# A gated recurrence on one core: the low fp16 parts come from a scan instead of a subtraction

## The chip, the cores and the metric
One core of a Trainium2 chip runs the whole program. The metric is the device time in microseconds, the median of several runs. Times of single instructions come from one profiled execution. PE is TensorE, DVE is VectorE, ACT is the Scalar engine, POOL is GpSimd and SP is SyncE.

## The reference
Two layers with residual sums. The first reduces to a factor per channel, since its transform is inverted exactly: `x` becomes `x * (2 + gate)`. The second is a gated recurrence over 2048 places of two sequences, 512 channels wide. What is computed in each of the 2048 steps:

```python
z = sigmoid(xz[t] + h @ U_z + vz)
r = sigmoid(xr[t] + h @ U_r + vr)
hh = tanh(xh[t] + r * h @ U + vh)        # (r * h) @ U
h = (1.0 - z) * h + z * hh
out[t] = x[t] + h
```

## The kernel before, in words
Channels lie on the 128 partitions in K = 4 chunks, B = 2 sequences each, so a state vector is 8 numbers per partition (S = 8). It is handled in two halves of four (HS = 4, two chunks). The projections of x are made in blocks of TB = 64 steps, one block ahead, and lie in `xp`.

The recurrent products are fp16. Every fp32 value is split in a high and a low fp16 part, weights and state both. The new state is kept as the sum of two vectors, `keep = (1-z) * h` and `zn = z * tanh`, each with its own two parts, so that the product of the next r and z need not wait for their sum. `h_part` holds four parts per value, `rh_part` two. A product (`tile_product`, L252) has 128 x 128 weights and 32 streamed columns: the parts of one chunk, repeated until 32 columns are full (`WIDE`). Its sums fall into a slot of the PSUM bank. The projection of x is put into the slot's last columns by the Scalar engine (`seed`, L335 and L337). VectorE then adds up the columns of a slot (`total`, L487).

A step runs like this. PE: 32 products for r, 32 for z, 32 for h. The r products take the first half of `h_part` first (12 products) and then wait for the second half (`hs0`, `hs1`); the h products do the same with `rh_part` (`rh0`, `rh1`). DVE: reduce r; for each half `(tanh+1)*h` into fp16 (L496), the same again in fp32 (L500), and their difference, the low part (L505); reduce z and h; `keep` and its parts (L522, L523, L527); for each half `z_mul * tanh` into fp16 (L532), the same in fp32 (L536), and the low part (L541); last `h_cur = keep + zn` (L553). ACT: the tanh of each sum (L351), the copy of the state into `hist` (L363), two linear functions of z (L368, L369), the three seeds.

The order on each engine is the order of the code; engines meet by counting semaphores, and an engine also waits for its own earlier result by a semaphore. The 2048 steps are 32 blocks; a block is 4 steps with the turn of the block (`make_out`, L564, behind the first; `make_y`, L455, behind the third) and then 12 rounds of a loop with 5 steps. In each round DVE stores one slice of the next projection behind the fourth step (`store_projection`, L558), 384 times in all; its addresses depend on the round, so register instructions (L557, L558) stand ahead of it.

Of the kernel before, what the change touches and what calls it, by code (L numbers as in the profile page):

```python
# [5 lines left out]
ALU = mybir.AluOpType  # L6
# [7 lines left out]
P = 128  # L14
# [5 lines left out]
def gru_kernel(nc, x, cond, W1, b1, W2, b2, W_z, U_z, C_z, b_z, W_r, U_r, C_r, b_r, W, U, C, b, out):  # L20
# [14 lines left out]

    WIDE = 32
    SLOT = WIDE + B
    KEEP, NEW = 0, PARTS
# [7 lines left out]
    with ExitStack() as ctx:  # L46
# [54 lines left out]
        ps_r, ps_h = ([pair[:, hf, :] for hf in range(2)] for pair in (pair_r, pair_h))  # L101
        SUM, TANH = 256, 384

        def cols(bank, g, m0, m1):
            slots = bank[:, SLOT * m0:SLOT * m1].rearrange("p (m c) -> p m c", c=SLOT)
            return slots[:, :, SLOT - ADDENDS[g] * B:SLOT].rearrange("p m (a b) -> p m a b", b=B)

# [64 lines left out]
        @block.gpsimd  # L172
        def _(pool):
            nc.gpsimd.memset(ident[:, :], 0.0).then_inc(s["ident_zero"], 1)
            pool.wait_ge(s["ident_zero"], 1)
            nc.gpsimd.affine_select(out=ident[:, :], in_=ident[:, :], compare_op=ALU.not_equal, fill=1.0,
                                    base=0, pattern=[[-1, P]], channel_multiplier=1).then_inc(s["ident_ok"], 1)

            nc.gpsimd.memset(h_cur[:, :], 0.0)
            nc.gpsimd.memset(hist[:, TB:2 * TB, :], 0.0)  # L180
            nc.gpsimd.memset(y_cur[:, :, :], 0.0)
            nc.gpsimd.memset(h_part[:, 0:HC], 0.0).then_inc(s["hs0"], 1)
            nc.gpsimd.memset(h_part[:, HC:K], 0.0).then_inc(s["hs1"], 1)
            nc.gpsimd.memset(xp[:, :, TB:2 * TB, :], 0.0).then_inc(s["h0_ready"], 1)
            pool.wait_ge(s["umax_ok"], G)
            nc.gpsimd.partition_all_reduce(u_all[:, :], u_max[:, :], P, RMAX).then_inc(s["uall_ok"], 1)

        @block.tensor
        def _(pe):
# [57 lines left out]
            def tile_product(bank, m, g, gm, k, parts, first):  # L247

                n = (ADDENDS[g] - 1) * B
                moving = parts[:, k, :, :].rearrange("p a b -> p (a b)").unsqueeze(1).broadcast_to([P, WIDE // n, n])  # L250
                for part in range(PARTS):
                    last = nc.tensor.matmul(bank[:, SLOT * m:SLOT * m + WIDE].rearrange("p (r n) -> p r n", n=n),  # L252
                                            u_part[:, g, part, k, gm * P:(gm + 1) * P], moving,
                                            start=first and part == 0, stop=False, skip_group_check=True)
                return last
# [65 lines left out]
        def _(act):  # L321
# [9 lines left out]
            def seed(banks, g, at):  # L331

                src = xp[:, g * K:(g + 1) * K, at, :]
                if g == Z:
                    return A(cols(banks, Z, 0, K)[:, :, ADDENDS[Z] - 1, :], src, ACT.Copy)  # L335
                to = banks[:, :, 0:SLOT * HC].rearrange("p h (m c) -> p h m c", c=SLOT)
                return A(to[:, :, :, WIDE:SLOT], src.rearrange("p (h m) b -> p h m b", h=2), ACT.Copy)  # L337

# [14 lines left out]
            def steps(t0, count, ring, turn=None):  # L353

                for u in range(count):
# [7 lines left out]
                    A(hist[:, prv, :], h_cur[:, :], ACT.Copy)  # L363
                    tanh(th_z[:, :], ps_z, Z, S, "z_sum", t1, "z_th")
# [25 lines left out]
            act.wait_ge(s["h_ok"], T)  # L390
            A(hist[:, (T - 1) % (2 * TB), :], h_cur[:, :], ACT.Copy).then_inc(s["copied"], 1)
            put_out(NB + 1)

        @block.vector
        def _(dve):
# [94 lines left out]
            def step(t1):  # L490
                kc = (slice(0, HC), slice(HC, K))


                def gated_high(hf):
                    dve.wait_ge(s[f"r{hf}_th"], t1)
                    V.scalar_tensor_tensor(rh_part[:, kc[hf], 0, :], kb(ps_r[hf][:, TANH:TANH + HS]), 1.0,  # L496
                                           kb(h_cur[:, half[hf]]), ALU.add, ALU.mult)

                def gated_full(hf):
                    V.scalar_tensor_tensor(rh[:, half[hf]], ps_r[hf][:, TANH:TANH + HS], 1.0, h_cur[:, half[hf]],  # L500
                                           ALU.add, ALU.mult).then_inc(s[f"rh32_{hf}"], 1)

                def gated_low(hf):
                    dve.wait_ge(s[f"rh32_{hf}"], t1)
                    V.tensor_tensor(rh_part[:, kc[hf], 1, :], kb(rh[:, half[hf]]), rh_part[:, kc[hf], 0, :],  # L505
                                    ALU.subtract).then_inc(s[f"rh{hf}"], 1)

                for hf in range(2):
                    dve.wait_ge(s[f"r{hf}_mm"], t1)
                    total(ps_r[hf], R, HC, f"r{hf}_sum")  # L510

                for hf in range(2):
                    gated_high(hf)
                    gated_full(hf)
# [7 lines left out]
                V.tensor_tensor(h_part[:, :, KEEP, :], kb(z_keep[:, :]), kb(h_cur[:, :]), ALU.mult)  # L522
                V.tensor_tensor(keep[:, :], z_keep[:, :], h_cur[:, :], ALU.mult).then_inc(s["keep_ok"], 1)  # L523

                def keep_low():
                    dve.wait_ge(s["keep_ok"], t1)
                    V.tensor_tensor(h_part[:, :, KEEP + 1, :], kb(keep[:, :]), h_part[:, :, KEEP, :], ALU.subtract)  # L527


                def new_high(hf):  # L530
                    dve.wait_ge(s[f"h{hf}_th"], t1)
                    V.tensor_tensor(h_part[:, kc[hf], NEW, :], kb(z_mul[:, half[hf]]),  # L532
                                    kb(ps_h[hf][:, TANH:TANH + HS]), ALU.mult)

                def new_full(hf):
                    V.tensor_tensor(zn[:, half[hf]], z_mul[:, half[hf]], ps_h[hf][:, TANH:TANH + HS],  # L536
                                    ALU.mult).then_inc(s[f"zn{hf}"], 1)
# [77 lines left out]
```

## Time and profile before

| | us |
|---|---|
| median of 3 runs | 6809.69 (6809.19 to 6810.33) |
| profiled execution, its time | 6811.76 |
| profiled execution, its span | 6809.9 |
| PE busy with products | 5998.4 (88%) |
| DVE busy | 4955.6 (73%) |
| ACT busy | 3331.6 (49%) |
| TensorE clock granted, mean | 0.996 of full speed |

Busy time is counted per engine as the time in which at least one of its instructions is under way. Instructions of one engine overlap: the next starts some 70 to 80 ns after the one before, while each lasts 150 ns or more, so a share of 73% does not mean that a quarter of the time is free for more of them. An instruction that needs the result of the one before has to wait for its end.

### The profile page before, as it was taken

How to read it: one execution, taken by the hardware profiler on the slowest of the kernel's cores; microseconds unless marked ns; L12 is line 12 of the kernel's file. 1: busy time of each engine (PE TensorE's matmuls, PEld its weight loads, DVE VectorE, ACT ScalarE, POOL GpSimd, SP SyncE). 2: the span in 40 equal slices, each digit the busy share in tenths (PEclk: the TensorE clock that was granted, in tenths of full speed). 3: DMA queues.
4: the chain of work that ended last, by engine and by line, in shares of the span. 5: the costliest groups of instructions: out<-in, count | busy, mean ns of one | idle time of the engine just before them, and what ended most of it. 6: DMA issues, size and time to landing. Idle time of an engine off the chain costs nothing.

```text
span 6809.9 us, 488240 instructions
## 1 busy us (share of the span) xinstructions
PE 5998.4 (88%) x200232; PEld 5642.2 (83%) x200232; DVE 4955.6 (73%) x43503; ACT 3331.6 (49%) x22603; POOL 3.5 (0%) x13
## 2 busy tenths in 40 slices
PE   7888888888888888888888888888888888888888
PEld 7888888888888888888888888888888888888888
DVE  5777777777777777777777777777777777777777
ACT  3444444444444444444444444444444444444444
POOL 0000000000000000000000000000000000000000
PEclk8999999999999999999999999999999999999999
DMA  2000000000000000000000000000000000000000
GB/s 84 17 18 15 18 17 18 17 17 17 18 17 18 15 18 17 18 18 15 18 17 18 17 18 15 18 17 18 17 17 17 18 17 18 15 18 18 17 18 15
DMA packets 80315, 129.97 MB, mean 19 GB/s; under 512 B 12336, under 2 KB 18480, under 8 KB 80304
## 3 DMA queue, kind: packets, MB, share of 16 engines
q1 hardware_dynamic: 80304, 129.81, 5.5%
q8 instruction: 8, 0.13, 0.0%
q14 instruction: 3, 0.02, 0.0%
HBM read 20.46 MB, written 8.65 MB: 4 GB/s over the span
## 4 chain that ended last, share of the span: by engine, by line
PE 71%; DVE 26%; issue 3%; SPq 0%; DMA 0%; ACT 0%; ACTq 0%; DVEq 0%
PE pair_r L252 30%; PE ps_z L252 24%; PE pair_h L252 17%; DVE pair_h L487 8%; DVE h_part L522 5%; DVE h_part L541 4%; DVE h_part L527 2%; DVE keep L523 2%; DVE zn L536 2%; DVE h_part L532 2%; PE ps_z L212 0%; DMA u_raw<-in_L_cond_U 0%; PE ps_o L212 0%; DVE u_max L424 0%; PE ps_x L224 0%
## 5 line engine op out<-in xcount | busy, mean ns | idle before, releaser
L252 PEld LDWEIGHTS pair_r<-h_part,u_part 128*128 128x128 f16 x65536 | 1845.1, 96 | 1119.9 <-DVE h_part L541 1115.8
L252 PE MATMUL pair_r<-h_part,u_part 128*128 128x32 f16 x65536 | 2048.7, 177 | 771.1 <-DVE h_part L541 758.6
L252 PE MATMUL pair_h<-rh_part,u_part 128*128 128x32 f16 x65536 | 2016.6, 177 | 12.5 <-DVE rh_part L505 12.5
L252 PE MATMUL ps_z<-h_part,u_part 128*128 128x32 f16 x65536 | 1961.5, 176 | 0.0
L252 PEld LDWEIGHTS pair_h<-rh_part,u_part 128*128 128x128 f16 x65536 | 1842.8, 96 | 17.3 <-DVE rh_part L505 15.7
L252 PEld LDWEIGHTS ps_z<-h_part,u_part 128*128 128x128 f16 x65536 | 1795.3, 95 | 0.0
L487 DVE TENSOR_REDUCE pair_r<-pair_r 128x4 f32<-128x20 f32 x4096 | 759.4, 186 | 818.1 <-PE pair_r L252 615.1
L351 ACT ACTIVATE pair_r<-pair_r 128x4 f32<-128x4 f32 x4096 | 644.8, 158 | 1445.1 <-DVE pair_r L487 1182.4
L487 DVE TENSOR_REDUCE pair_h<-pair_h 128x4 f32<-128x12 f32 x4096 | 717.7, 175 | 665.7 <-PE pair_h L252 665.7
L351 ACT ACTIVATE th_z<-ps_z 128x8 f32<-128x8 f32 x2048 | 364.1, 178 | 1046.0 <-DVE ps_z L487 1046.0
L337 ACT ACTIVATE pair_h<-xp 128x8 f32 (+1 forms) x2049 | 369.9, 181 | 807.8 <-DVE zn L536 807.8
L505 DVE TENSOR_TENSOR rh_part<-rh,rh_part 128x4 f16<-128x4 f32 x4096 | 662.2, 162 | 141.1
L541 DVE TENSOR_TENSOR h_part<-zn,h_part 128x4 f16<-128x4 f32 x4096 | 669.6, 163 | 70.5
L224 PE MATMUL ps_p<-y_next,w_stage 128*128 128x128 f32 x3072 | 718.1, 316 | 0.0
L351 ACT ACTIVATE pair_h<-pair_h 128x4 f32<-128x4 f32 x4096 | 647.2, 158 | 102.2
L496 DVE SCALAR_TENSOR_TENSOR rh_part<-pair_r,h_cur 128x4 f16<-128x4 f32 x4096 | 649.6, 159 | 6.0
L532 DVE TENSOR_TENSOR h_part<-z_mul,pair_h 128x4 f16<-128x4 f32 x4096 | 625.6, 153 | 0.0
L500 DVE SCALAR_TENSOR_TENSOR rh<-pair_r,h_cur 128x4 f32<-128x4 f32 x4096 | 621.8, 152 | 0.0
L536 DVE TENSOR_TENSOR zn<-z_mul,pair_h 128x4 f32<-128x4 f32 x4096 | 619.8, 151 | 0.0
L224 PEld LDWEIGHTS ps_p<-y_next,w_stage 128*128 128x128 f32 x3072 | 458.2, 188 | 0.0
L363 ACT ACTIVATE hist<-h_cur 128x8 f32 x2048 | 428.2, 209 | 4.4
L487 DVE TENSOR_REDUCE ps_z<-ps_z 128x8 f32<-128x40 f32 x2048 | 421.8, 206 | 0.0
(70 smaller groups left out, 3275.9 us busy)
## 6 DMA issues: line engine op xcount, KB each, us to landing
w_stage<-w_in SPq DMA_DIRECT2D x384, 256.0 KB, 2.3
x_tok<-in_x SPq DMA_DIRECT2D x68, 128.0 KB, 2.6
out_dram<-o_tok SPq DMA_DIRECT2D x66, 128.0 KB, 2.3
mlp_w<-in_L_cond_W SPq DMA_DIRECT2D x2, 1024.0 KB, 6.9
u_raw<-in_L_cond_U_r SPq DMA_DIRECT2D x1, 1024.0 KB, 5.6
u_raw<-in_L_cond_U_z SPq DMA_DIRECT2D x1, 1024.0 KB, 7.6
u_raw<-in_L_cond_U SPq DMA_DIRECT2D x1, 1024.0 KB, 10.3
w_in<-in_L_cond_W_r SPq DMA_DIRECT2D x4, 256.0 KB, 9.8
```

The lines of the kernel that those rows point to most:

```text
L224: return nc.tensor.matmul(bank[:, col:col + P], weight[:, k, :], y_next[:, k * B:(k + 1) * B, :].rearrange("p b t -> p (b t)"), start=(k = ...
L252: last = nc.tensor.matmul(bank[:, SLOT * m:SLOT * m + WIDE].rearrange("p (r n) -> p r n", n=n), u_part[:, g, part, k, gm * P:(gm + 1) * P] ...
L337: return A(to[:, :, :, WIDE:SLOT], src.rearrange("p (h m) b -> p h m b", h=2), ACT.Copy)
L351: A(to, bank[:, SUM:SUM + n], ACT.Tanh, scale=scale_reg[g]).then_inc(s[done], 1)
L363: A(hist[:, prv, :], h_cur[:, :], ACT.Copy)
L487: return V.tensor_reduce(bank[:, SUM:SUM + m * B].rearrange("p (m b) -> p m b", b=B), cols(bank, g, 0, m).rearrange("p m a b -> p m b a"), ...
L496: V.scalar_tensor_tensor(rh_part[:, kc[hf], 0, :], kb(ps_r[hf][:, TANH:TANH + HS]), 1.0, kb(h_cur[:, half[hf]]), ALU.add, ALU.mult)
L500: V.scalar_tensor_tensor(rh[:, half[hf]], ps_r[hf][:, TANH:TANH + HS], 1.0, h_cur[:, half[hf]], ALU.add, ALU.mult).then_inc(s[f"rh32_{hf}" ...
L505: V.tensor_tensor(rh_part[:, kc[hf], 1, :], kb(rh[:, half[hf]]), rh_part[:, kc[hf], 0, :], ALU.subtract).then_inc(s[f"rh{hf}"], 1)
L532: V.tensor_tensor(h_part[:, kc[hf], NEW, :], kb(z_mul[:, half[hf]]), kb(ps_h[hf][:, TANH:TANH + HS]), ALU.mult)
L536: V.tensor_tensor(zn[:, half[hf]], z_mul[:, half[hf]], ps_h[hf][:, TANH:TANH + HS], ALU.mult).then_inc(s[f"zn{hf}"], 1)
L541: V.tensor_tensor(h_part[:, kc[hf], NEW + 1, :], kb(zn[:, half[hf]]), h_part[:, kc[hf], NEW, :], ALU.subtract).then_inc(s[f"hs{hf}"], 1)
```

## The change
The low part is no longer made from a full fp32 product minus the high part. Three places (a step of the scan each) stand for one value. A scan runs over them: state = state * factor - subtrahend. For the new state the factors of one value are 0, tanh and z_mul, and the subtrahends are -1, 0 and the high part, so that the states are 1, tanh and tanh * z_mul - high. For the gated state they are 0, tanh, h and -1, -1, high, which gives (tanh + 1) * h - high. The parts keep this layout in memory: `part_of` is a part with 12 places of one half, of which every third holds a value. `h_cur` and `z_mul` become columns of the factor arrays `r_scan` and `n_scan`, and the tanh results go there, into SBUF instead of PSUM. The fp32 `rh` is gone. `zn` is made once in full behind the last scan, and `h_cur` waits for it. A product streams 8 neighbouring places of each part, of which two hold values (places 2 and 5 of 8); a slot is 40 columns wide, and `total` and `seed` pick columns 2 and 5 of each run of 8. ACT's seed of `pair_h` no longer waits for `zn1`.

```diff
-    WIDE = 32
-    SLOT = WIDE + B
+    STEP, RUN, WIDE = 3, 8, 32
+    SLOT = WIDE + RUN
+    PITCH = HS * STEP
...
+        r_scan = sb("r_scan", [P, S, STEP])
+        n_scan = sb("n_scan", [P, S, STEP])
+        h_cur, z_mul = r_scan[:, :, STEP - 1], n_scan[:, :, STEP - 1]
+        h_part = sb("h_part", [P, 2 * 2 * PARTS * PITCH + RUN], F16)
+        rh_part = sb("rh_part", [P, 2 * PARTS * PITCH + RUN], F16)
...
         def cols(bank, g, m0, m1):
-            slots = bank[:, SLOT * m0:SLOT * m1].rearrange("p (m c) -> p m c", c=SLOT)
-            return slots[:, :, SLOT - ADDENDS[g] * B:SLOT].rearrange("p m (a b) -> p m a b", b=B)
+            runs = bank[:, SLOT * m0:SLOT * m1].rearrange("p (m a c) -> p m a c", c=RUN, m=m1 - m0)
+            return runs[:, :, SLOT // RUN - ADDENDS[g]:, STEP - 1:STEP * B:STEP]
...
+        def part_of(parts, count, hf, part):
+            at = (hf * count + part) * PITCH
+            return parts[:, at:at + PITCH]
+        def place(parts, count, hf, part, step=STEP - 1):
+            return part_of(parts, count, hf, part).rearrange("p (s c) -> p s c", c=STEP)[:, :, step]
...
-                n = (ADDENDS[g] - 1) * B
-                moving = parts[:, k, :, :].rearrange("p a b -> p (a b)").unsqueeze(1).broadcast_to([P, WIDE // n, n])
+                n = ADDENDS[g] - 1
+                at = k // HC * n * PITCH + k % HC * B * STEP
+                runs = parts[:, at:at + n * PITCH].rearrange("p (a c) -> p a c", c=PITCH)[:, :, 0:RUN]
+                moving = runs.unsqueeze(1).broadcast_to([P, WIDE // (n * RUN), n, RUN])
...
-                        tanh(ps_r[hf][:, TANH:TANH + HS], ps_r[hf], R, HS, f"r{hf}_sum", t1, f"r{hf}_th")
+                        tanh(r_scan[:, half[hf], 1], ps_r[hf], R, HS, f"r{hf}_sum", t1, f"r{hf}_th")
...
-                    tanh(ps_h[1][:, TANH:TANH + HS], ps_h[1], H, HS, "h1_sum", t1, "h1_th")
-                    act.wait_ge(s["zn1"], t1)
+                    tanh(n_scan[:, half[1], 1], ps_h[1], H, HS, "h1_sum", t1, "h1_th")
                     seed(pair_h, H, nxt)
...
+                def low(parts, count, hi, hf, factors, done):
+                    V.tensor_tensor_scan(part_of(parts, count, hf, hi + 1), factors[:, half[hf]].rearrange("p s c -> p (s c)"),
+                                         part_of(parts, count, hf, hi), 0.0, ALU.mult, ALU.subtract).then_inc(s[done], 1)
...
-                def gated_full(hf):
-                    V.scalar_tensor_tensor(rh[:, half[hf]], ps_r[hf][:, TANH:TANH + HS], 1.0, h_cur[:, half[hf]],
-                                           ALU.add, ALU.mult).then_inc(s[f"rh32_{hf}"], 1)
...
                 new_high(0)
-                new_full(0)
                 keep_low()
                 new_low(0)
                 new_high(1)
-                new_full(1)
                 new_low(1)
-                V.tensor_tensor(h_cur[:, :], keep[:, :], zn[:, :], ALU.add).then_inc(s["h_ok"], 1)
+                V.tensor_tensor(zn[:, :], z_mul, n_scan[:, :, 1], ALU.mult).then_inc(s["zn_ok"], 1)
+                dve.wait_ge(s["zn_ok"], t1)
+                V.tensor_tensor(h_cur, keep[:, :], zn[:, :], ALU.add).then_inc(s["h_ok"], 1)
```

VectorE from the reduction of the second half of h to the next step, in the step with `store_projection`, before (ISA and REGISTER_ALU are register instructions):

```order
L487 TENSOR_REDUCE pair_h<-pair_h 128x4 [waits s_h1_mm]
L532 TENSOR_TENSOR h_part<-z_mul,pair_h 128x2x2 [waits s_h0_th]
L536 TENSOR_TENSOR zn<-z_mul,pair_h 128x4
L527 TENSOR_TENSOR h_part<-keep,h_part 128x4x2 [waits s_keep_ok]
L541 TENSOR_TENSOR h_part<-zn,h_part 128x2x2 [waits s_zn0]
L532 TENSOR_TENSOR h_part<-z_mul,pair_h 128x2x2 [waits s_h1_th]
L536 TENSOR_TENSOR zn<-z_mul,pair_h 128x4
L541 TENSOR_TENSOR h_part<-zn,h_part 128x2x2 [waits s_zn1]
L553 TENSOR_TENSOR h_cur<-keep,zn 128x8
L557 ISA
L558 ISA [waits s_proj_mm]
L558 TENSOR_TENSOR xp<-ps_p,v_bias 128x2x64
```

The same place after the change (the scans are listed as SCALAR_TENSOR_TENSOR of L522, `h_cur` as r_scan, tanh and `z_mul` as n_scan):

```order
L514 TENSOR_REDUCE pair_h<-pair_h 128x4 [waits s_h1_mm]
L557 TENSOR_TENSOR h_part<-n_scan 128x4 [waits s_h0_th]
L552 TENSOR_TENSOR h_part<-keep,h_part 128x2x4 [waits s_keep_ok]
L522 SCALAR_TENSOR_TENSOR h_part<-n_scan,h_part 128x12 [waits s_nhi0]
L557 TENSOR_TENSOR h_part<-n_scan 128x4 [waits s_h1_th]
L522 SCALAR_TENSOR_TENSOR h_part<-n_scan,h_part 128x12 [waits s_nhi1]
L571 TENSOR_TENSOR zn<-n_scan 128x8
L573 TENSOR_TENSOR r_scan<-keep,zn 128x8 [waits s_zn_ok]
L577 ISA
L578 ISA [waits s_proj_mm]
L578 TENSOR_TENSOR xp<-ps_p,v_bias 128x2x64
```

Two instructions of four elements are gone, one of eight has come behind the second scan, and the sum `h_cur` (L553, now L573) has got a wait for it, with the register instructions behind.

VectorE in the same step, the r gate, before (`rh_part` is what the h products wait for):

```order
L496 SCALAR_TENSOR_TENSOR rh_part<-pair_r,h_cur 128x2x2 [waits s_r0_th]
L500 SCALAR_TENSOR_TENSOR rh<-pair_r,h_cur 128x4
L505 TENSOR_TENSOR rh_part<-rh,rh_part 128x2x2 [waits s_rh32_0]
L496 SCALAR_TENSOR_TENSOR rh_part<-pair_r,h_cur 128x2x2 [waits s_r1_th]
L500 SCALAR_TENSOR_TENSOR rh<-pair_r,h_cur 128x4
L505 TENSOR_TENSOR rh_part<-rh,rh_part 128x2x2 [waits s_rh32_1]
```

And after:

```order
L527 SCALAR_TENSOR_TENSOR rh_part<-r_scan 128x4 [waits s_r0_th]
L522 SCALAR_TENSOR_TENSOR rh_part<-r_scan,rh_part 128x12 [waits s_rhi0]
L527 SCALAR_TENSOR_TENSOR rh_part<-r_scan 128x4 [waits s_r1_th]
L522 SCALAR_TENSOR_TENSOR rh_part<-r_scan,rh_part 128x12 [waits s_rhi1]
```

Each half has one instruction less; the scan waits for the fp16 high part instead of the fp32 product.

## Rows read from the trace of the kernel before

**Rows 1.** Section 4 of the page: the chain that ended last, by engine and line

```profile
PE 71%; DVE 26%; issue 3%; SPq 0%; DMA 0%; ACT 0%; ACTq 0%; DVEq 0%
```

**Rows 2.** Waits: who waited for whom, us in total, times, longest us

```profile
PE pair_r L252 <- DVE h_part L541: 758.6, 1983, 0.7
```

**Rows 3.** Timeline of a step: start, length (us), engine, line, instruction [idle before <- releaser]

```profile
3001.89 1.00 PE L252 MATMUL pair_r<-h_part,u_part 128*128 128x32 f16 x32 [0.65 <-DVE h_part L541]
...
3004.59 0.17 DVE L487 TENSOR_REDUCE pair_h<-pair_h 128x4 f32<-128x12 f32 x1
...
3004.80 0.16 ACT L351 ACTIVATE pair_h<-pair_h 128x4 f32<-128x4 f32 x1
...
3004.92 0.16 DVE L541 TENSOR_TENSOR h_part<-zn,h_part 128x4 f16<-128x4 f32 x1
...
3005.14 1.00 PE L252 MATMUL pair_r<-h_part,u_part 128*128 128x32 f16 x32 [0.31 <-DVE h_part L541]
3005.26 0.16 DVE L541 TENSOR_TENSOR h_part<-zn,h_part 128x4 f16<-128x4 f32 x1
...
3005.35 0.18 ACT L337 ACTIVATE pair_h<-xp 128x8 f32 x1 [0.39 <-DVE zn L536]
...
3005.99 0.96 PE L252 MATMUL ps_z<-h_part,u_part 128*128 128x32 f16 x32
...
3006.29 0.16 DVE L496 SCALAR_TENSOR_TENSOR rh_part<-pair_r,h_cur 128x4 f16<-128x4 f32 x1
...
3006.56 0.16 DVE L505 TENSOR_TENSOR rh_part<-rh,rh_part 128x4 f16<-128x4 f32 x1
...
3006.80 0.85 PE L252 MATMUL pair_h<-rh_part,u_part 128*128 128x32 f16 x27
```

**Rows 4.** Groups of instructions by form: busy us, mean ns | idle before

```profile
L252 PE MATMUL pair_r<-h_part,u_part 128*128 128x32 f16 x65536 | 2048.7, 177 | 771.1 <-DVE h_part L541 758.6 <-issue 3.9
L252 PE MATMUL pair_h<-rh_part,u_part 128*128 128x32 f16 x65536 | 2016.6, 177 | 12.5 <-DVE rh_part L505 12.5
...
L487 DVE TENSOR_REDUCE pair_h<-pair_h 128x4 f32<-128x12 f32 x4096 | 717.7, 175 | 665.7 <-PE pair_h L252 665.7
L541 DVE TENSOR_TENSOR h_part<-zn,h_part 128x4 f16<-128x4 f32 x4096 | 669.6, 163 | 70.5
L351 ACT ACTIVATE pair_h<-pair_h 128x4 f32<-128x4 f32 x4096 | 647.2, 158 | 102.2
...
L487 DVE TENSOR_REDUCE ps_z<-ps_z 128x8 f32<-128x40 f32 x2048 | 421.8, 206 | 0.0
L351 ACT ACTIVATE th_z<-ps_z 128x8 f32<-128x8 f32 x2048 | 364.1, 178 | 1046.0 <-DVE ps_z L487 1046.0
...
L564 DVE SCALAR_TENSOR_TENSOR oT<-hist,y_cur 128x512 f32<-128x512 f32 x33 | 35.8, 1085 | 0.4 <-ACT hist L391 0.4
L455 DVE TENSOR_TENSOR y_next<-ps_x,gate 128x512 f32<-128x512 f32 x33 | 22.6, 684 | 0.2 <-PE ps_x L194 0.2
```

**Rows 5.** Timeline of a step with L558 behind it

```profile
3014.92 1.00 PE L252 MATMUL pair_r<-h_part,u_part 128*128 128x32 f16 x32 [0.30 <-DVE h_part L541]
3015.03 0.16 DVE L541 TENSOR_TENSOR h_part<-zn,h_part 128x4 f16<-128x4 f32 x1
3015.11 0.16 DVE L553 TENSOR_TENSOR h_cur<-keep,zn 128x8 f32<-128x8 f32 x1
...
3015.51 0.29 DVE L558 TENSOR_TENSOR xp<-ps_p,v_bias 128x128 f32 x1 [0.24 <-issue]
3015.72 0.42 DVE L487 TENSOR_REDUCE pair_r<-pair_r 128x4 f32<-128x20 f32 x2
...
3018.26 0.32 PE L252 MATMUL pair_r<-h_part,u_part 128*128 128x32 f16 x6 [0.64 <-DVE h_part L541]
```

**Rows 6.** Register instructions of L557 and L558 there: count, ns min/median/max, first and last start

```profile
L557 DVEq FUSED_REGOPS  x1: 114/114/114, 3015.0 to 3015.0; - x1
...
L558 DVEq FUSED_REGOPS  x2: 52/112/173, 3015.2 to 3015.4; - x2
```

More of the change, by code:

```diff
@@ L121, in gru_kernel, with keep_place @@
         half = (slice(0, HS), slice(HS, S))
+        by_half = lambda a: a.rearrange("p (h s) -> p h s", h=2)
+        def part_of(parts, count, hf, part):
[3 more added lines that the diff above has]
+            return part_of(parts, count, hf, part).rearrange("p (s c) -> p s c", c=STEP)[:, :, step]
+        def keep_place(low):
+            both = h_part[:, 0:2 * 2 * PARTS * PITCH].rearrange("p (h a s c) -> p h a s c", h=2, a=2 * PARTS, c=STEP)
+            return both[:, :, KEEP + low, :, STEP - 1]
         BYTES = 16 * B
@@ L177, in _ @@
                                     base=0, pattern=[[-1, P]], channel_multiplier=1).then_inc(s["ident_ok"], 1)
-            nc.gpsimd.memset(h_cur[:, :], 0.0)
+            nc.gpsimd.memset(r_scan[:, :, :], 0.0)
+            nc.gpsimd.memset(n_scan[:, :, :], 0.0)
+            nc.gpsimd.memset(rh_part[:, :], 0.0).then_inc(s["rh_zero"], 1)
+            nc.gpsimd.memset(h_part[:, :], 0.0).then_inc(s["scan_zero"], 1)
+            pool.wait_ge(s["rh_zero"], 1)
+            for hf in range(2):
+                for step in range(STEP - 1):
+                    nc.gpsimd.memset(place(rh_part, PARTS, hf, 0, step), -1.0)
             nc.gpsimd.memset(hist[:, TB:2 * TB, :], 0.0)
             nc.gpsimd.memset(y_cur[:, :, :], 0.0)
-            nc.gpsimd.memset(h_part[:, 0:HC], 0.0).then_inc(s["hs0"], 1)
-            nc.gpsimd.memset(h_part[:, HC:K], 0.0).then_inc(s["hs1"], 1)
+            pool.wait_ge(s["scan_zero"], 1)
+            for hf in range(2):
+                nc.gpsimd.memset(place(h_part, 2 * PARTS, hf, NEW, 0), -1.0).then_inc(s[f"hs{hf}"], 1)
             nc.gpsimd.memset(xp[:, :, TB:2 * TB, :], 0.0).then_inc(s["h0_ready"], 1)
@@ L247, in tile_product @@
             def tile_product(bank, m, g, gm, k, parts, first):
[L249 to L250 removed]
+                n = ADDENDS[g] - 1
+                at = k // HC * n * PITCH + k % HC * B * STEP
+                runs = parts[:, at:at + n * PITCH].rearrange("p (a c) -> p a c", c=PITCH)[:, :, 0:RUN]
+                moving = runs.unsqueeze(1).broadcast_to([P, WIDE // (n * RUN), n, RUN])
                 for part in range(PARTS):
[L252 removed]
+                    last = nc.tensor.matmul(bank[:, SLOT * m:SLOT * m + WIDE].rearrange("p (r a c) -> p r a c", a=n, c=RUN),
                                             u_part[:, g, part, k, gm * P:(gm + 1) * P], moving,
@@ L336, in seed @@
                 to = banks[:, :, 0:SLOT * HC].rearrange("p h (m c) -> p h m c", c=SLOT)
-                return A(to[:, :, :, WIDE:SLOT], src.rearrange("p (h m) b -> p h m b", h=2), ACT.Copy)
+                return A(to[:, :, :, WIDE + STEP - 1:WIDE + STEP * B:STEP],
+                         src.rearrange("p (h m) b -> p h m b", h=2), ACT.Copy)
             act.wait_ge(s["h0_ready"], 1)
@@ L360, in steps @@
                     for hf in range(2):
-                        tanh(ps_r[hf][:, TANH:TANH + HS], ps_r[hf], R, HS, f"r{hf}_sum", t1, f"r{hf}_th")
-                    A(hist[:, prv, :], h_cur[:, :], ACT.Copy)
+                        tanh(r_scan[:, half[hf], 1], ps_r[hf], R, HS, f"r{hf}_sum", t1, f"r{hf}_th")
+                    A(hist[:, prv, :], h_cur, ACT.Copy)
                     tanh(th_z[:, :], ps_z, Z, S, "z_sum", t1, "z_th")
@@ L368, in steps @@
                     A(z_keep[:, :], th_z[:, :], ACT.Copy, scale=-0.5, bias=0.5).then_inc(s["z_keep"], 1)
-                    A(z_mul[:, :], th_z[:, :], ACT.Copy, scale=H_SCALE / 2, bias=H_SCALE / 2)
-                    tanh(ps_h[0][:, TANH:TANH + HS], ps_h[0], H, HS, "h0_sum", t1, "h0_th")
+                    A(z_mul, th_z[:, :], ACT.Copy, scale=H_SCALE / 2, bias=H_SCALE / 2)
+                    tanh(n_scan[:, half[0], 1], ps_h[0], H, HS, "h0_sum", t1, "h0_th")
                     seed(ps_z, Z, nxt)
-                    tanh(ps_h[1][:, TANH:TANH + HS], ps_h[1], H, HS, "h1_sum", t1, "h1_th")
-                    act.wait_ge(s["zn1"], t1)
+                    tanh(n_scan[:, half[1], 1], ps_h[1], H, HS, "h1_sum", t1, "h1_th")
                     seed(pair_h, H, nxt)
@@ L390, in _ @@
             act.wait_ge(s["h_ok"], T)
-            A(hist[:, (T - 1) % (2 * TB), :], h_cur[:, :], ACT.Copy).then_inc(s["copied"], 1)
+            A(hist[:, (T - 1) % (2 * TB), :], h_cur, ACT.Copy).then_inc(s["copied"], 1)
             put_out(NB + 1)
@@ L490, in step @@
             def step(t1):
-                kc = (slice(0, HC), slice(HC, K))
+                def low(parts, count, hi, hf, factors, done):
+                    V.tensor_tensor_scan(part_of(parts, count, hf, hi + 1), factors[:, half[hf]].rearrange("p s c -> p (s c)"),
+                                         part_of(parts, count, hf, hi), 0.0, ALU.mult, ALU.subtract).then_inc(s[done], 1)
                 def gated_high(hf):
                     dve.wait_ge(s[f"r{hf}_th"], t1)
-                    V.scalar_tensor_tensor(rh_part[:, kc[hf], 0, :], kb(ps_r[hf][:, TANH:TANH + HS]), 1.0,
-                                           kb(h_cur[:, half[hf]]), ALU.add, ALU.mult)
-                def gated_full(hf):
-                    V.scalar_tensor_tensor(rh[:, half[hf]], ps_r[hf][:, TANH:TANH + HS], 1.0, h_cur[:, half[hf]],
-                                           ALU.add, ALU.mult).then_inc(s[f"rh32_{hf}"], 1)
+                    V.scalar_tensor_tensor(place(rh_part, PARTS, hf, 0), r_scan[:, half[hf], 1], 1.0,
+                                           h_cur[:, half[hf]], ALU.add, ALU.mult).then_inc(s[f"rhi{hf}"], 1)
                 def gated_low(hf):
-                    dve.wait_ge(s[f"rh32_{hf}"], t1)
-                    V.tensor_tensor(rh_part[:, kc[hf], 1, :], kb(rh[:, half[hf]]), rh_part[:, kc[hf], 0, :],
-                                    ALU.subtract).then_inc(s[f"rh{hf}"], 1)
+                    dve.wait_ge(s[f"rhi{hf}"], t1)
+                    low(rh_part, PARTS, 0, hf, r_scan, f"rh{hf}")
                 for hf in range(2):
@@ L513, in step @@
                     gated_high(hf)
-                    gated_full(hf)
                     gated_low(hf)
@@ L521, in step @@
                 dve.wait_ge(s["z_keep"], t1)
-                V.tensor_tensor(h_part[:, :, KEEP, :], kb(z_keep[:, :]), kb(h_cur[:, :]), ALU.mult)
-                V.tensor_tensor(keep[:, :], z_keep[:, :], h_cur[:, :], ALU.mult).then_inc(s["keep_ok"], 1)
+                V.tensor_tensor(keep_place(0), by_half(z_keep[:, :]), by_half(h_cur), ALU.mult)
+                V.tensor_tensor(keep[:, :], z_keep[:, :], h_cur, ALU.mult).then_inc(s["keep_ok"], 1)
                 def keep_low():
                     dve.wait_ge(s["keep_ok"], t1)
-                    V.tensor_tensor(h_part[:, :, KEEP + 1, :], kb(keep[:, :]), h_part[:, :, KEEP, :], ALU.subtract)
+                    V.tensor_tensor(keep_place(1), by_half(keep[:, :]), keep_place(0), ALU.subtract)
                 def new_high(hf):
                     dve.wait_ge(s[f"h{hf}_th"], t1)
[L532 to L537, printed above, removed]
+                    V.tensor_tensor(place(h_part, 2 * PARTS, hf, NEW), z_mul[:, half[hf]],
+                                    n_scan[:, half[hf], 1], ALU.mult).then_inc(s[f"nhi{hf}"], 1)
                 def new_low(hf):
-                    dve.wait_ge(s[f"zn{hf}"], t1)
-                    V.tensor_tensor(h_part[:, kc[hf], NEW + 1, :], kb(zn[:, half[hf]]), h_part[:, kc[hf], NEW, :],
-                                    ALU.subtract).then_inc(s[f"hs{hf}"], 1)
+                    dve.wait_ge(s[f"nhi{hf}"], t1)
+                    low(h_part, 2 * PARTS, NEW, hf, n_scan, f"hs{hf}")
                 dve.wait_ge(s["h1_mm"], t1)
```

9 lines of the change are left out of this document (2 added, 7 removed).

## The prediction
> **What bounds the kernel now.** Read the chain of waits first [rows 1]: TensorE holds 71% of it and VectorE 26%, and nearly all of it lies in the recurrence, so this is a loop of 2048 dependent steps and no engine is full. The waits say where the loop closes: the r products wait for VectorE L541, 1983 times and 758.6 us in all, 0.37 us a step [rows 2]. L541 is the low-part subtraction that the change replaces.
>
> The timeline of a step [rows 3] gives the lengths. The r products start at 3001.89 and again at 3005.14, so a step is 3.25 to 3.26 us. Between them the PE runs 32 r, 32 z and 32 h products. z takes 3005.99 to 3006.80, 0.81 us, which is 25 ns a product; r takes 0.85. The 0.04 more are two short waits in r: one after its first product, one at the thirteenth, where the second half's L541 is needed. That L541 starts at 3005.26, ends 0.16 later and reaches the PE 0.06 later (the first L541, 3004.92, ends at 5.08, and r starts at 5.14), so at 3005.48; undisturbed, the thirteenth product would be due 0.31 after 3005.14 (the first takes 0.04, eleven more 25 ns each), at 3005.45. The second half therefore closes the loop, and what is gained there is gained in all 2048 steps: the time is linear in it.
>
> The page's other stretch is a step in which VectorE does something besides the step [rows 5]. Behind the last L541 (3015.03) and h_cur (3015.11) stands L558, which starts only at 3015.51, after 0.24 us of "issue". The next reduction of r comes at 3015.72 instead of 0.07 earlier, and the next r products start at 3018.26, not 3.26 but 3.34 us after 3014.92. This happens 384 times.
>
> **Low part by scan.** In the second half now: reduce h1, tanh, high part (L532), the fp32 copy (L536), 0.03 of semaphore, L541. After: reduce, tanh, high part, semaphore, scan. L536 leaves; but the fp16 high part is now what the scan waits for. Step by step from rows 3 and 4:
> - The reduction L487 starts at 3004.59 behind L522 and L523, which now read h_cur with a gap of two words. L564 reads hist in steps of eight words and takes 1085 ns, L455 reads straight and takes 684 ns, both for 512 elements: hopping costs up to 0.78 ns an element. Sixteen elements of two instructions make at most 12 ns, no gap makes 0; I take 8. Start at 4.60.
> - L487 lasts 0.17 and tanh starts at 4.77+0.03, as now (4.80). Its target moves from PSUM to SBUF. The nearest rows are th_z (178 ns, 8 elements, into SBUF) and the same tanh into PSUM (158 ns, 4 elements); take 3 ns off for the elements and it is 16 dearer, between 0 and 20. tanh ends at 4.60+0.17+0.03+0.175 = 4.98 (unrounded).
> - High part at 5.01; both inputs are in SBUF, as in L541, hence its 163 ns. Its result is usable at 5.01+0.165+0.035 = 5.21.
> - Scan of 12 elements. No row shows one. Lower end: L541's 163 plus eight more elements at the reduction's slope ((206-175)/28 = 1.1 ns) = 172. Upper end: 12 places that each cost a triple pass, like the 40-element reduction: 206. Each place multiplies, then subtracts, and the next needs the result, so I count twice 1.1 ns: 163-4+26 = 185, which is also near the middle.
> - Scan ends at 5.21+0.185 = 5.40, and the PE has it at 5.455. Now it is 5.48. Gain 25 ns a step, 2048 x 25 = 51 us. The ends of the scan alone make it 78 us (172) and 8 us (206).
> The Trainium skill, "DVE: opcode table, instruction layouts, handler registers and perf-mode slots", section Datapath and trigger behaviour, says that the built-in scan runs at half throughput because its feedback costs bubble cycles. By that rule the scan would be 163-4 plus 12 times two cycles, 184 ns, and the sum within 2 us of mine; a rule at full rate would give 172. No row here shows a scan.
>
> The first half is not the limit: its high part is issued 0.08 behind the reduction (the spacing of L541 and h_cur in rows 5), at 4.68; 0.20 later, 4.88, its scan starts, ends at 5.065, r starts at 5.125, and the thirteenth product would be due 0.31 later, at 5.435, still before 5.455. The r gate has cover: rh must reach the PE at 3006.80; L496 at 6.29 becomes 6.31 (tanh into SBUF), +0.20, +0.185, +0.06 = 6.75, now 6.56+0.16+0.06 = 6.78. The reset of pair_h loses its wait (ACT L337 at 3005.35 behind L536); the Scalar engine then waits for r anyway, so nothing is gained. The POOL memsets and the other layout lie in the prologue, beside it: 0.
>
> **What moves late.** The fp32 product zn is no longer a by-product. Now h_cur is issued 0.08 behind the last L541 and waits for nothing. After the change the full zn (8 elements) comes 0.08 behind the last scan, and h_cur waits for it (s_zn_ok): 0.08+0.165+0.03 = 0.28 behind the scan. In 2048 steps that alone is hidden, since r's reduction is due some 0.6 us behind L541 (3015.65 against 3015.03, [rows 5]). Not hidden is what is queued behind h_cur. For L558 these are three register instructions (114, 173 and 52 ns, [rows 6]). Their first starts at 3015.0, before h_cur at 3015.11: they run past h_cur while it stands in the queue, but not past L541, which waits for a semaphore. In the same way the Scalar engine's L337, which needs a register instruction after its wait for L536, starts at 3005.35, while L541, which waits for the same and needs none, is at 3005.26. So I take it that a register instruction is held behind an instruction that waits. Then the registers start with h_cur, not with L541: from L541 to L558 it is 0.48 now; from the scan it will be 0.28+0.47 = 0.75, so 0.27 more, and the scan starts 0.045 earlier than L541: L558 comes 0.225 later on the clock. Against a step that is due 0.025 earlier, that is 0.25 later, on top of the 0.07 that L558 holds r's reduction up already: 0.32. Take off the 0.05 of cover of the r gate, and 0.27 goes through to the next step; today 0.085 does (3.34 against 3.25 to 3.26), so 0.18 more. 384 x 0.18 = 69 us. Behind make_out and make_y (L564 and L455, 33 each, of which 32 stand in the loop) the same thing happens: 64 x 0.18 = 12 us.
>
> **Sum.** Profiled execution 6811.8 us (span 6809.9 and 1.9 around it): -51 +69 +12 = +30, 6842. The three timed runs have their median 2 us lower, 6809.7: 6840 us.
>
> **Rivals.**
> (a) Faster: the register instructions run while h_cur waits. Then L558 comes out as now, and the loss is gone: 6810-51+2 = 6761 us. For it: nothing shows an instruction with a wait as the second in the queue. Against: rows 3 and 6 as above. A variant ends the same way: the loss is there but the scan costs under 165 ns.
> (b) Slower by more: strides in PSUM. All reductions now read in steps of eight words where they read in steps of two. If these cost 0.78 ns an element as in SBUF, the z reduction (40 elements, on the loop) costs 31 ns and h's (12) 9: 2048 x 40 = +82 on top of the forecast, 6922 us. For it: L564. Against: the reductions read in steps of two words already, never two neighbours in a row, and go at 1.1 ns. The Trainium skill, "PSUM — Partial Sum Buffer", section Specifications (TRN2), gives cachelines of 8 bytes and says non-contiguous patterns slow matmuls; by it the old pattern would be as bad as the new, and the time would not change; the trace's 1.1 ns agrees that two-word steps are free.
> (c) The products slow down: each now streams four runs of 8 places that begin at multiples of 12 bytes. If each took 1 ns more, the 52 products from r's thirteenth to z's last cost 52 ns a step: +106 on top, 6946 us. Against: a product of 32 columns takes 177 ns for runs of 8 (r) and for runs of 4 (h) alike [rows 4].
> (d) No change: the scan at its lower end, 172: -78+81 = +3, 6813 us.
>
> **Chances.** Forecast mechanism 0.60 (own range 6813 to 6883, -78 or -8 for the scan's ends and +81), a 0.13, b 0.13, c 0.04, d 0.10. The range of 8 in 10 reaches from 6785 (a is left out) to 6930 (c is left out). About 0.2%, 14 us, can be told from no change. Faster: a and a little of the mix, 0.18. Within: d and the lower part of the forecast, 0.22. Slower: 0.60.
>
> **What would show it.** Right: a scan of about 185 ns; the r products 3.23 us apart in plain steps; in the steps behind L558 (new number L578) some 3.49 us; h_cur about 0.28 behind the last scan, and L578 about 0.47 behind h_cur. Wrong: a scan over 206 ns, which alone makes every step longer; a z reduction over 220 ns (b); products further apart than 25 ns (c); L578 less than 0.2 behind h_cur (a).

## The result and the profile after

The changed kernel takes 6909.5 us (median of 4 runs, 6906.99 to 6911.27) against 6809.9 before: 1.0145 times, 95% interval 1.013 to 1.0161. It is slower, by 99.6 us. The forecast was +30 us, 6840, with a range from 6785 to 6930: the side was right, the size was three times too small.

The forecast's own terms first. The groups of instructions after, with the columns of [rows 4]:

```profile
L279 PE MATMUL pair_r<-h_part,u_part 128*128 128x32 f16 x65536 | 2059.7, 179 | 672.4 <-DVE h_part L522 664.8 <-issue 3.9
L279 PE MATMUL pair_h<-rh_part,u_part 128*128 128x32 f16 x65536 | 1984.6, 179 | 68.0 <-DVE rh_part L522 13.7
...
L522 DVE TENSOR_TENSOR_SCAN h_part<-n_scan,h_part 128x12 f16<-128x12 f32 x4096 | 749.8, 183 | 70.0
...
L514 DVE TENSOR_REDUCE pair_h<-pair_h 128x4 f32<-128x12 f32 x4096 | 722.2, 176 | 678.3 <-PE pair_h L279 678.3
L379 ACT ACTIVATE n_scan<-pair_h 128x4 f32<-128x4 f32 x4096 | 718.5, 175 | 140.1
...
L514 DVE TENSOR_REDUCE ps_z<-ps_z 128x8 f32<-128x40 f32 x2048 | 410.5, 200 | 1.3
```

The scan takes 183 ns (estimated 185), tanh into SBUF 175 (estimated 158+16). The reductions in eight-word steps are no dearer: 176 and 200 ns against 175 and 206 in [rows 4].

A plain step and the step behind L578, timeline (start, length, engine, line, instruction):

```profile
3001.83 1.01 PE L279 MATMUL pair_r<-h_part,u_part 128*128 128x32 f16 x32 [0.30 <-DVE h_part L522]
...
3005.06 1.01 PE L279 MATMUL pair_r<-h_part,u_part 128*128 128x32 f16 x32 [0.30 <-DVE h_part L522]
...
3008.30 1.01 PE L279 MATMUL pair_r<-h_part,u_part 128*128 128x32 f16 x32 [0.30 <-DVE h_part L522]
3008.40 0.18 DVE L522 TENSOR_TENSOR_SCAN h_part<-n_scan,h_part 128x12 f16<-128x12 f32 x1
3008.50 0.15 DVE L571 TENSOR_TENSOR zn<-n_scan 128x8 f32<-128x8 f32 x1
3008.68 0.17 DVE L573 TENSOR_TENSOR r_scan<-keep,zn 128x8 f32<-128x8 f32 x1
...
3009.16 0.29 DVE L578 TENSOR_TENSOR xp<-ps_p,v_bias 128x128 f32 x1 [0.31 <-issue]
3009.37 0.26 DVE L514 TENSOR_REDUCE pair_r<-pair_r 128x4 f32<-128x20 f32 x2
...
3011.80 0.99 PE L279 MATMUL pair_r<-h_part,u_part 128*128 128x32 f16 x32 [0.60 <-DVE h_part L522]
```

Plain steps are 3.23 us, as forecast. h_cur (now named r_scan, L573) comes 0.28 behind the scan, L578 comes 0.48 behind h_cur, the first of its register instructions starts with h_cur (row below; 14 ns behind it in every round of the trace, 64 ns ahead of it in the kernel before), and the step takes 3008.30 to 3011.80, 3.50 us (forecast 3.49); [rows 5] had 3.34.

```profile
L577 DVEq FUSED_REGOPS  x1: 114/114/114, 3008.7 to 3008.7; - x1
```

What the forecast did not have follows one step later, at the head of the loop. The timeline goes on, with the register instructions of VectorE's loop (L604) below it:

```profile
3011.89 0.18 DVE L522 TENSOR_TENSOR_SCAN h_part<-n_scan,h_part 128x12 f16<-128x12 f32 x1
...
3012.18 0.17 DVE L573 TENSOR_TENSOR r_scan<-keep,zn 128x8 f32<-128x8 f32 x1
...
3012.73 0.29 DVE L514 TENSOR_REDUCE pair_r<-pair_r 128x4 f32<-128x20 f32 x2 [0.39 <-PE pair_r L279]
```

```profile
L604 DVEq ALU_OP  x1: 40/40/40, 3012.2 to 3012.2; - x1
L604 DVEq COMPARE_BRANCH  x1: 56/56/56, 3012.3 to 3012.3; - x1
L604 DVEq FUSED_REGOPS  x1: 139/139/139, 3012.5 to 3012.5; - x1
```

In a plain step the reduction comes 0.75 us behind the r products (3005.81 against 3005.06 in the trace), here 0.93 (3012.73 against 3011.80). The branch stands behind h_cur as L578 does; the next register instruction starts 0.29 us behind the branch's start, lasts 0.14, and only then comes the reduction. In the kernel before, the step that starts at 3001.89 in [rows 3] is such a head; its branch and third register instruction are the rows below, with the same 0.29 between their starts, and its reduction comes at 3002.62, 0.73 behind the products as in any step. There the branch had just enough time.

```profile
L584 DVEq COMPARE_BRANCH  x1: 56/56/56, 3002.1 to 3002.1; - x1
L584 DVEq FUSED_REGOPS  x1: 139/139/139, 3002.4 to 3002.4; - x1
```

Then the clock. The mean granted clock is 0.937 of full speed, 0.996 before. Three stretches of TensorE, columns: us, busy us (and count) of PE, PEld, DVE, ACT, POOL, granted clock, DMA:

```profile
3041.90:3045.31 3.41, 2.69 (x99) 2.48 (x96) 2.44 (x20) 1.51 (x11) 0.00 (x0) 1.00 0.20 77
3045.31:3048.73 3.42, 3.42 (x104) 3.13 (x102) 2.38 (x19) 1.60 (x11) 0.00 (x0) 0.50 0.00 0
3048.73:3062.38 13.65, 12.03 (x415) 11.26 (x412) 10.09 (x74) 6.11 (x44) 0.00 (x0) 1.00 0.00 0
```

The stretch ahead of the fall holds the step behind L578, with PE busy 2.69 of 3.41 us. Then the clock is at its lower level, 1.2 instead of 2.4 GHz, for 3.4 us. There are 241 stretches at this level in the trace, nearly all of 3.4 us, against 3 before. 215 of them begin in the step right behind a step with L578: 184 at the head of the loop, and 31 in the first step of a block. A product takes 188 ns in them instead of 177, and a 128-column fp32 one 492 instead of 316. A step at the loop's head takes 3.40 us where the clock is at its lower level for a part of it (207 of 384) and 3.36 where it is not, and the step behind it 3.25 and 3.20.

From the start of the r products of all steps, the 99 us come together like this (mean ns of a step, and us for all of its kind):

| step of a round | count | before | after | us |
|---|---|---|---|---|
| third and fourth | 768 | 3258 | 3235 | -18 |
| fifth, behind the store | 383 | 3341 | 3510 | +65 |
| first, head of the loop | 384 | 3258 | 3385 | +49 |
| second | 384 | 3258 | 3227 | -12 |
| four at the block's turn | 128 | | | +15 |

### The profile page after: what moved, and what is told of

Read it like the earlier page. It is cut to its first block, busy times and chain, and to the rows that moved or that the text cites. A ratio compares the mean times of both kernels' runs of the same rounds, so it can differ in the third digit from the quotient of the medians.

```text
span 6909.4 us, 482103 instructions
## 1 busy us (share of the span) xinstructions
PE 6143.6 (89%) x200232; PEld 5706.4 (83%) x200232; DVE 5107.5 (74%) x37359; ACT 3188.9 (46%) x22603; POOL 3.8 (0%) x20
## 4 chain that ended last, share of the span: by engine, by line
PE 62%; DVE 30%; issue 5%; DVEq 1%; ACT 1%; SPq 0%; DMA 0%
PE pair_r L279 23%; PE ps_z L279 19%; PE pair_h L279 18%; DVE pair_h L514 7%; DVE h_part L522 5%; DVE h_part L547 4%; DVE h_part L557 3%; DVE h_part L552 2%; PE ps_p L249 2%; DVE keep L548 2%; DVE rh_part L522 1%; DVE pair_r L514 1%; DVEq L578 1%; ACT r_scan L379 1%; DVE rh_part L527 1%
## 5 line engine op out<-in xcount | busy, mean ns | idle before, releaser
L379 ACT ACTIVATE r_scan<-pair_r 128x4 f32<-128x4 f32 x4096 | 653.9, 176 | 2405.7 <-DVE pair_r L514 2250.7
L522 DVE TENSOR_TENSOR_SCAN rh_part<-r_scan,rh_part 128x12 f16<-128x12 f32 x4096 | 748.6, 183 | 140.2
L522 DVE TENSOR_TENSOR_SCAN h_part<-n_scan,h_part 128x12 f16<-128x12 f32 x4096 | 749.8, 183 | 70.0
L379 ACT ACTIVATE n_scan<-pair_h 128x4 f32<-128x4 f32 x4096 | 718.5, 175 | 140.1
L527 DVE SCALAR_TENSOR_TENSOR rh_part<-r_scan 128x4 f16<-128x4 f32 x4096 | 681.3, 166 | 120.7 <-ACT r_scan L379 74.9
L557 DVE TENSOR_TENSOR h_part<-n_scan 128x4 f16<-128x4 f32 x4096 | 684.5, 167 | 0.0
L391 ACT ACTIVATE hist<-r_scan 128x8 f32 x2048 | 435.7, 213 | 2.8
L397 ACT ACTIVATE n_scan<-th_z 128x8 f32<-128x8 f32 x2048 | 401.9, 196 | 0.0
L573 DVE TENSOR_TENSOR r_scan<-keep,zn 128x8 f32<-128x8 f32 x2048 | 349.5, 171 | 70.5
L396 ACT ACTIVATE z_keep<-th_z 128x8 f32<-128x8 f32 x2048 | 393.7, 192 | 0.0
```

What stands on the lines that cost most here:

```text
L379: A(to, bank[:, SUM:SUM + n], ACT.Tanh, scale=scale_reg[g]).then_inc(s[done], 1)
L391: A(hist[:, prv, :], h_cur, ACT.Copy)
L397: A(z_mul, th_z[:, :], ACT.Copy, scale=H_SCALE / 2, bias=H_SCALE / 2)
L522: V.tensor_tensor_scan(part_of(parts, count, hf, hi + 1), factors[:, half[hf]].rearrange("p s c -> p (s c)"), part_of(parts, count, hf, hi ...
L527: V.scalar_tensor_tensor(place(rh_part, PARTS, hf, 0), r_scan[:, half[hf], 1], 1.0, h_cur[:, half[hf]], ALU.add, ALU.mult).then_inc(s[f"rh ...
L557: V.tensor_tensor(place(h_part, 2 * PARTS, hf, NEW), z_mul[:, half[hf]], n_scan[:, half[hf], 1], ALU.mult).then_inc(s[f"nhi{hf}"], 1)
```

## The experiments

**The full zn ahead of the last scan.** The scan waits 0.2 us for its high part; zn fits in there.

```diff
-                new_low(1)
                 V.tensor_tensor(zn[:, :], z_mul, n_scan[:, :, 1], ALU.mult).then_inc(s["zn_ok"], 1)
+                new_low(1)
                 dve.wait_ge(s["zn_ok"], t1)
```

> The changed kernel with the full fp32 zn issued ahead of the last scan, in the shadow of the scan's own wait, so that h_cur's wait is met when its turn comes. Theory (register instructions are held behind h_cur's unmet wait, at L578 and at the head of the loop, and the longer TensorE pauses bring the half clock): both costs vanish, 2048 steps gain 25 ns each, 6755 to 6785 us, granted clock back at 0.99 or more, steps behind the store below 3.35 us. Rival (the hopping strides, the new streams or the scan bring the half clock by themselves): plain steps stay at 3.23, but the clock stays near 0.94 and the time above 6800 us.

Measured: 6739.9 us against 6804.9, ratio 0.9903 (0.9887 to 0.992): faster than both, and 15 us below the expected range. Its timeline:

```profile
3005.37 0.16 DVE L570 TENSOR_TENSOR zn<-n_scan 128x8 f32<-128x8 f32 x1
3005.39 1.01 PE L279 MATMUL pair_r<-h_part,u_part 128*128 128x32 f16 x32 [0.29 <-DVE h_part L522]
3005.49 0.18 DVE L522 TENSOR_TENSOR_SCAN h_part<-n_scan,h_part 128x12 f16<-128x12 f32 x1
3005.59 0.15 DVE L573 TENSOR_TENSOR r_scan<-keep,zn 128x8 f32<-128x8 f32 x1
...
3008.62 1.01 PE L279 MATMUL pair_r<-h_part,u_part 128*128 128x32 f16 x32 [0.30 <-DVE h_part L522]
```

h_cur is 0.10 behind the scan instead of 0.28, plain steps are 3.23 as in the changed kernel, the step behind the store is 3.30, the head of the loop has no excess (3.21), the clock is 0.996. The steps behind the store gain 42 ns on the kernel before and the heads 46, where plain steps gain the expected 25; why these two gain more was not tried. One instruction in another place takes back all that the change lost; scan, layout and strides are cleared.

**The wait alone.** As above, but h_cur waits for the last scan, which it does not need.

```diff
+                t2 = dve.snap(t1 + 1)
                 dve.wait_ge(s["z_mm"], t1)
...
+                V.tensor_tensor(zn[:, :], z_mul, n_scan[:, :, 1], ALU.mult)
                 new_low(1)
-                dve.wait_ge(s["zn_ok"], t1)
+                dve.wait_ge(s["hs1"], t2)
```

> As the one before, but h_cur waits for the end of the last scan, which it does not need: no instruction is added on VectorE's queue behind the scan, only a wait. Theory (held register instructions): they start 0.22 us behind the scan's start instead of some 0.28 in the changed kernel, so most of the cost is back: 6835 to 6870 us. Rival (the later place of zn and h_cur in VectorE's queue costs, not the wait): as without the wait, 6755 to 6785 us.

Measured: 6849.2 us, ratio 1.0063 (1.0047 to 1.008). Against the kernel without this wait that is 109 us for a wait: behind the scan stands h_cur, as there. The wait's value `t2` costs a register instruction, which runs not where the code has it but directly ahead of h_cur:

```profile
3005.90 0.18 DVE L522 TENSOR_TENSOR_SCAN h_part<-n_scan,h_part 128x12 f16<-128x12 f32 x1
3006.12 0.17 DVE L574 TENSOR_TENSOR r_scan<-keep,zn 128x8 f32<-128x8 f32 x1
```

```profile
L573 DVEq ALU_OP  x1: 40/40/40, 3005.9 to 3005.9; - x1
```

It starts with the scan and lasts 40 ns, so it is over more than 0.1 us before h_cur starts, and h_cur starts when the scan has ended: the register instruction delays nothing. Steps behind the store 3.44, loop heads 3.32, clock 0.944. The place of zn in the queue is not the cause; the wait is.

**No store.** Left out is the store of the projections after the first block, so that all later blocks use old ones.

```diff
                     if proj is not None and u == K - 1:
-                        store_projection(*proj)
+                        pass
```

> The changed kernel without store_projection (L578 and its three register instructions); left out is the store of the projections after the first block, so all later blocks use old ones. Theory: the steps behind the store fall from 3.51 to about 3.23 us (0.276 x 384 = 106 us), the head of the loop still costs some 0.13 us a round: 6785 to 6815 us. Rival (the head of the loop is only late because the step before was late): its excess goes too, 6740 to 6765 us.

Measured: 6815.2 us, ratio 1.0014 (1.0004 to 1.0023), at the upper edge of the expectation. The steps behind the store fall to 3.28 and the heads of the loop keep 3.38: the second cost stands on its own. I had expected 3.23. The trace shows where the 0.05 comes from: the register instruction that the Scalar engine has ahead of its seed of `pair_r` takes 60 ns in a plain step and 110 ns in the last step of a round (rows below), and the seed, `z_keep` and what follows them come 50 ns later. The clock is 0.964.

```profile
L364 ACTq FUSED_REGOPS  x1: 60/60/60, 3039.5 to 3039.5; - x1
```

```profile
L364 ACTq FUSED_REGOPS  x1: 110/110/110, 3046.0 to 3046.0; - x1
```

**The wait in the kernel before.** No scan, no new layout.

```diff
+                t2 = dve.snap(t1 + 1)
                 dve.wait_ge(s["z_mm"], t1)
...
                 new_low(1)
+                dve.wait_ge(s["hs1"], t2)
                 V.tensor_tensor(h_cur[:, :], keep[:, :], zn[:, :], ALU.add).then_inc(s["h_ok"], 1)
```

> The kernel before, with one wait more: h_cur waits for the end of the last low part, which it does not need. No scan, no new layout. Theory (held register instructions): they start 0.19 us later, which costs 0.15 us in each step behind the store and 0.10 at each loop head, 384 of each, and 10 us at the block turns: 6900 to 6940 us. Rival (the wait costs nothing, the loss of the changed kernel is due to zn's place or the new layout): 6808 to 6825 us.

Measured: 6962.9 us, ratio 1.0229 (1.0212 to 1.0246): +158, beyond the expected +90 to +130. Its plain steps:

```profile
3006.53 1.00 PE L252 MATMUL pair_r<-h_part,u_part 128*128 128x32 f16 x32 [0.30 <-DVE h_part L542]
3006.65 0.16 DVE L542 TENSOR_TENSOR h_part<-zn,h_part 128x4 f16<-128x4 f32 x1
3006.84 0.17 DVE L555 TENSOR_TENSOR h_cur<-keep,zn 128x8 f32<-128x8 f32 x1
...
3009.79 1.00 PE L252 MATMUL pair_r<-h_part,u_part 128*128 128x32 f16 x32 [0.31 <-DVE h_part L542]
```

h_cur is 0.19 behind the low part instead of 0.08, and plain steps keep their 3.26: the wait costs nothing there. The steps behind the store take 3.53 (+0.19, I had +0.15), the heads of the loop 3.40 (+0.14, I had +0.10), and the clock is 0.935, which I had not priced. So the larger cost does not need the change at all.

**Filling TensorE's pause.** The fifth step of a round has no projection product; two are put there, into an unused bank.

```diff
+                        if u == K:
+                            projection(ps_x, 0, w_in[:, 0], 0)
+                            projection(ps_x, 0, w_in[:, 0], K - 1)
```

> The changed kernel with two more 128-column fp32 products into an unused bank behind the h products of the fifth step of each round, which has none, beside VectorE's work. Theory (the half clock follows TensorE's longer pauses and costs some 20 us of the 100): clock 0.98 or more, 6880 to 6895 us at a before of 6810, the steps at the loop's head 3.36 us. Rival (the half clock costs most of what the forecast missed, 50 us or more): 6830 to 6860 us. If it does not bring the clock back, the pause that counts is the one ahead of the h products, and the time stays near 6909.

Measured: 6892.9 us, ratio 1.0124 (1.0108 to 1.0141), clock 0.987, against the changed kernel's 1.0145. Each against its own runs of the kernel before, that is +85 us where the changed kernel has +100, so adding work to TensorE makes the kernel some 15 us faster; the two intervals overlap a little, but the traces agree: heads fall from 3385 to 3366 ns and the steps behind them from 3227 to 3198, 18 us in all, while the other steps of a round stay within 2 ns and the block turns the same in sum. Of the stretches at the lower clock 41 are left. None begins behind a step that was filled; all but one of those in the recurrence begin at the block's turn, in its four steps or the one behind them. So the half clock follows the pauses (the length of a pause and the work missing in it are not told apart here), and it is the smaller part of the miss.

**Filling both pauses**, with one more product ahead of the h products of that step.

```diff
+                    if proj is not None and u == K:
+                        nc.tensor.matmul(ps_x[:, P:2 * P], w_in[:, 0, 0, :], y_next[:, 0:B, :].rearrange("p b t -> p (b t)"),
+                                         start=True, stop=True)
                     staggered(ps_h, H, rh_part, "rh", "h", t1)
```

> As the one before, with one more such product ahead of the h products of the same step, in the pause of 0.3 us that the late r gate leaves. Theory: the pause there is filled too, the clock is back at 0.99 if it was not already, and the time is within 10 us of the kernel with the first filling or below it, 6880 to 6895 us. Rival: the clock does not depend on these pauses: 0.94 and 6909 us.

Measured: 6889.8 us, ratio 1.0121 (1.0104 to 1.0138), clock 0.988: the same within the intervals. The second filling lengthens its own step (3.53 for 3.51) and brings no more clock. 37 low stretches are left, and but for one those in the recurrence again begin at the block's turn, where neither kernel fills anything; which pause there brings them stays open.

**VectorE's loop with two rounds in its body.**

```diff
-                with dve.Fori(0, GM) as i:
-                    steps(dve.snap(n * TB + i * BODY + TURN), BODY, proj=(dve.snap(n * GM + i + 2), i, other))
+                with dve.Fori(0, GM // 2) as j:
+                    for odd in range(2):
+                        i = dve.snap(j * 2 + odd)
+                        steps(dve.snap(n * TB + i * BODY + TURN), BODY, proj=(dve.snap(n * GM + i + 2), i, other))
```

> The changed kernel with VectorE's loop of 12 rounds written as 6 turns of two rounds; nothing else is changed. Theory (VectorE's loop branch and the register instruction behind it are held behind h_cur and make the first reduction of r 0.18 us late at each loop head): 192 of 384 such steps lose their excess, between 0.09 and 0.13 us each: 17 to 25 us less, and a part of the half clock with them, 6875 to 6895 us. Rival (the excess follows from the store one step earlier): 6905 to 6915 us.

Measured: 6982.3 us, ratio 1.0257 (1.024 to 1.0274), 87 us above the expected range. The part asked for came: the first steps of a round fall from 3385 to 3327 ns on average, 384 x 0.058 = 22 us, and where two rounds follow each other inside the body the head takes 3.26 us on average, against 3.40 at the others. The steps behind the store fall too in the second of the two rounds, to 3.44, which I had not forecast. But at the turn of each block stands this:

```profile
2227.11 0.17 DVE L573 TENSOR_TENSOR r_scan<-keep,zn 128x8 f32<-128x8 f32 x1
2227.58 0.96 PE L279 MATMUL ps_z<-h_part,u_part 128*128 128x32 f16 x32
2230.33 0.27 DVE L514 TENSOR_REDUCE pair_r<-pair_r 128x4 f32<-128x20 f32 x2 [3.05 <-issue]
```

VectorE issues nothing for 3.05 us, and the waits list 31 such cases:

```profile
DVE pair_r L514 <- issue: 95.7, 31, 3.3
```

The step that begins a block takes 6.83 instead of 3.64 us: 31 x 3.19 = 99 us. The queue that loads instructions points to the reason, first the changed kernel, then this one (packets, MB, share):

```profile
q14 instruction: 3, 0.02, 0.0%
```

```profile
q14 instruction: 159, 1.30, 0.1%
```

156 packets more: in the trace five of 8 KB stand behind each of the 31 turns, the first 1.0 us behind the outer branch, inside the pause, the last 49 us behind the start of the block. So code is loaded there that the changed kernel does not load. That the longer body pushed the start of the block's code out of reach, so that the outer branch has to load it again, is my reading of it.

## Why the prediction was wrong

- **Low part by scan.** Right: 183 ns for 185, and the plain step gains 23 to 25 ns for 25. The Trainium skill, "DVE: opcode table, instruction layouts, handler registers and perf-mode slots", Datapath and trigger behaviour, says that the built-in scan runs at half throughput. The forecast's estimate from it was 184, and the trace's 183 agrees.
- **What moves late, L578.** Right in mechanism and size: over a plain step 275 ns now against 83 before, 0.19 more, for 0.18; 74 us for 69. The kernel with the early zn shows that it was avoidable, the added wait in the kernel before that it is the wait.
- **The step that failed** is the sentence in this part that for the rest of the 2048 steps h_cur's delay "is hidden, since r's reduction is due some 0.6 us behind L541". I looked for what stands behind h_cur in the three places where a DVE instruction does, and not at the loop's own branch, which is held there too, 384 times. At a loop head the reduction is 0.18 late; over a plain step the head and the step after it together cost 142 ns, 384 x 0.142 = 55 us, where the sum had 0.
- **Inside these 55 us, and not in the sum at all, is the clock.** At full clock head and next step take 3362 and 3198 ns, 91 over two plain steps or 35 us; the other 20 us are the lower clock, and the filling gives back 15 to 18 of them. The page before shows 0.996, and I asked only whether products slow down by their stream (rival c), not what longer pauses of TensorE do to the granted clock. The rest of the miss is smaller: over plain steps the block turns cost 18 us for 12. The outer branch is held as well, and the first step of a block takes 3.64 us instead of 3.28; the clock falls in every one of them, and with the filling, where it stays full in them, they take 3.46. The sum as measured is -48 +74 +55 +18 = 99 us.
- **Rivals.** (a) is refuted: register instructions do not run while h_cur waits. (b) is refuted: the z reduction lasts 200 ns. (c) is refuted as told: at full clock the 31 intervals from the first to the last z product are 25 ns each as before; 179 ns instead of 177 is the half clock's share. (d) is refuted: the scan is not 172 but 183 ns, and the loss behind h_cur is larger.
- On (a) the Trainium skill, "Advanced Engine Details and Errata", Sequencer and Instruction Queues, says that the sequencer pushes an engine instruction into a queue, 8 deep for VectorE, where it waits for its semaphore, and that it executes a control instruction itself. Read so, the register instructions would have run on behind a waiting h_cur. Here they do not: L577's starts with h_cur, and a wait that nothing needs costs 109 us.

## What to carry to other kernels

On VectorE a wait costs more than its own instruction: the address arithmetic, the branch of the loop and the register instruction behind it are held with it. Here it takes 0.48 us from h_cur to the store behind it, and 0.55 from h_cur to the first reduction of the next round. Put the last instruction of a loop body so that its wait is already met, and move its producer into an earlier shadow. When a change lengthens a pause of TensorE, look at the granted clock as well as at the pause.

## What was not expected of the hardware

- A branch that is taken: 0.29 us from the start of VectorE's loop branch to the next register instruction, in the kernel before as in the changed one, though the branch itself lasts 56 ns. Where the loop ends and the branch is not taken, it is 0.09 us.
- VectorE issues nothing for 3.05 us at the outer branch once its loop holds two rounds, with 159 instruction packets instead of 3. The Trainium skill, "Runtime: NRT & Kernel Launch", Instruction fetch mechanics, says that a taken branch whose target is not in the loaded pages forces a fetch; the trace agrees and gives the price.
- Some 15 us less by more products: TensorE's clock is at its lower level in 241 stretches with longer pauses and in 41 when one of them is filled.
- VectorE reads PSUM in steps of eight words at the rate of steps of two (176 against 175 ns for 12 elements), while L564, which reads hist in SBUF in eight-word steps, takes 1085 ns against 684 of L455 [rows 4]. These are two different instructions, so the steps need not be the whole difference.
